# AdaLN-FFN kernel on one core: x of tiles 2 and 3 loaded ahead of the first product's weights, the mixing weights made per block, and the first phase's lists in that order

## The chip, the cores and the metric

The kernel runs on one core of a Trainium2 chip. The metric is the device time of one execution in microseconds (us). TensorE is called PE here, VectorE DVE, ScalarE ACT, GpSimd POOL and the engine that starts most transfers SP. PE runs at one of two clocks, 1.2 or 2.4 GHz; the profile gives the granted one as a share of 2.4 GHz.

## The reference

```
x = x + L0_ffn(L0_cond(x, cond, weight, c_weight, fside), ffn_weight)
x = x + L1_ffn(L1_cond(x, cond, W0, b0, W1, b1, W2, b2, weight, bias_k), kernel, scale)

L0_cond: grouped convolution over 512 positions (32 channels, 4 groups, 9 taps),
         plus cond @ c_weight.T, plus fside, one value for a channel
L0_ffn:  rows and weights rounded to int8 by their largest magnitude, product
         [.., 512] x [512, 512], times both scales
L1_cond: att = softmax(gelu(gelu(cond @ W0 + b0) @ W1 + b1) @ W2 + b2)   # 64 x 8
         agg_w = einsum('bk,koi->boi', att, weight)                      # 64 x 32 x 32
         out = einsum('boi,bih->boh', agg_w, x) + (att @ bias_k)[:, :, None]
L1_ffn:  scale * (out @ (kernel * 2 - 1)),  [512, 512] signs
```

x is 64 x 32 x 512 in float32, 4 MB, and so is the result.

## The kernel before

The 64 samples are worked on in 16 tiles `t` of four samples each, 128 rows of 512. A tile goes through these steps: convolution on PE (`conv`, line 361, always for two tiles at once, in five `conv_step`s of 16 matmuls), bias on ACT (`convolved`, L759), largest magnitudes and scales on DVE (`maxima` L606, `scales` L615 to L629), rounding on POOL (`quantise`, L862), turning on PE (`turn_tile`, L381) and a copy on ACT (`quantised`, L765), the int8 product on PE (`ffn0_tile`, L389), scaling on DVE (`dequantise`, L636), the sum with x on POOL (`first_sum`, L875), the mixing over channels on PE (`mix_tile`, L396) and its bias on DVE (L644), a split into a high and a low part (ACT L771, POOL L881), the product with the signs on PE (`ffn1_tile`, L404 and L407), the result on DVE (L651) and the store.

A first phase comes ahead of the loop. It makes the convolution's weights, the two small gelu layers (`hidden1`, `hidden2`), the softmax (`logits`, `attention`), the int8 weights of the first product (`ffn0_weights(a)` for a = 0 to 3: load, DVE L554, POOL L853, PE L313, ACT L737), their scales (`ffn0_scales`, L321 and L567), and `mix`, which holds for each tile a 128 x 128 matrix with four 32 x 32 blocks of `agg_w` on its diagonal. In the same phase the tiles 0 to 3 are convolved, and tiles 0 and 1 go on to `dequantise`. The loop `for t in range(4, NT + 5)` follows; on PE it begins with the convolution of tiles 4 and 5, behind waits for all copies into `mix`.

Every engine works its list in the order in which the code is written, and waits on semaphores. So the order of the calls sets what stands behind what. A load of x for a tile is two transfers, `load_x(t, 0)` and `load_x(t, 1)`, of 256 KB each (the second is the same data shifted by one position), `load_q(a)` is one of 256 KB.

In the kernel before, `mixing_weights` on PE is eight matmuls (L338) of a 128 column piece of `mixk` with all 64 columns of `att_T`. Their result stands in PSUM with the output channels spread over all 128 partitions, and is taken to `mix` in sixteen copies of 32 x 128: eight on DVE (L599) and, through a copy `agg_sb` by ACT (L748), eight on POOL (L898).

## Time and profile before

| | us |
|---|---|
| median of three runs | 126.05 (125.63 to 126.14) |
| the profiled execution, its own time | 127.2 |
| its span in the trace | 125.2 |
| PE busy | 114.5 (91% of the span) |
| DVE, ACT, POOL busy | 76.0, 41.9, 70.6 |
| granted PE clock, mean over the span | 0.944 |

All times of the trace are counted from the span's start. The own time of an execution is 2.0 us longer than its span. A float32 matmul is recorded as two passes, so 16 matmuls are 32 records, each with its own weight load. Some records of matmuls are missing, so an "x151" in the chain stands for 160 passes.

### The profile page before, as it was taken

To read this page: it belongs to the slowest core of one execution; us is meant where nothing else is said; L and a number is where in the kernel's file an instruction comes from. 1 tells how busy PE (TensorE), PEld (TensorE's weight loads), DVE (VectorE), ACT (ScalarE), POOL (GpSimd) and SP (SyncE) were. 2 spreads that over 40 slices of the span, in tenths; PEclk is the share of its full clock that TensorE was granted. 3 is DMA by queue.
4 is the path that set the end of the run, shared out by engine and by line. 5 is a ranking of instruction groups with operands and counts; after the bars stand their busy time and mean duration, and the time that the engine had idled before them with its cause. 6 is when DMAs were issued, how large, how long until landed. Compare 5 with 4: busy or idle time off the path is not lost.

```text
span 125.2 us, 4314 instructions
## 1 busy us (share of the span) xinstructions
PE 114.5 (91%) x1759; PEld 77.2 (62%) x1759; DVE 76.0 (61%) x189; ACT 41.9 (33%) x81; POOL 70.6 (56%) x102
## 2 busy tenths in 40 slices
PE   4978999998998894999999999999999998699990
PEld 1345545653665562677768667777777684587880
DVE  6270578825965990078819855982987278275532
ACT  0414154355357402524083126406331722420210
POOL 6970047557974776007852882677088407975640
PEclk9999559589999999599999999999999999999999
DMA  1898999995999988309394731505132251021024
GB/s 42 220 200 304 222 232 216 205 220 124 228 225 224 228 178 242 73 14 284 105 260 135 216 118 58 168 5 169 67 109 93 80 163 56 32 84 63 25 99 153
DMA packets 11378, 18.60 MB, mean 149 GB/s; under 512 B 1624, under 2 KB 2776, under 8 KB 11360
## 3 DMA queue, kind: packets, MB, share of 16 engines
q1 hardware_dynamic: 10512, 17.84, 54.0%
q10 hardware_dynamic: 560, 0.44, 1.9%
q8 instruction: 14, 0.23, 0.9%
q0 software_dynamic: 288, 0.06, 0.4%
q14 instruction: 4, 0.03, 0.1%
HBM read 14.12 MB, written 4.19 MB: 146 GB/s over the span
## 4 chain that ended last, share of the span: by engine, by line
PE 77%; DVE 6%; DMA 5%; issue 4%; ACTq 2%; POOL 2%; ACT 2%; POOLq 0%; DVEq 0%
PE ps L361 21%; PE ps L404 13%; PE ps L407 11%; PE ps L396 11%; PE ps L389 10%; DMA xs<-in_x_dram 5%; PE ps L381 4%; DVE q_max L554 2%; PE ps L338 2%; DVE mix L599 1%; PE ps L321 1%; ACT xq L765 1%; POOL x L875 1%; PE ps L313 1%; PE ps L423 1%
## 5 line engine op out<-in xcount | busy, mean ns | idle before, releaser
L875 POOL TENSOR_TENSOR x<-xr,delta 128x512 f32<-128x512 f32 x16 | 18.7, 1168 | 29.8 <-DVE delta L636 29.1
L361 PE MATMUL ps<-xs,conv_st 32*32 32x256 f32 x1280 | 31.5, 424 | 3.2 <-issue 1.8
L361 PEld LDWEIGHTS ps<-xs,conv_st 32*32 32x32 f32 x1280 | 17.3, 106 | 10.9 <-issue 5.4
L881 POOL TENSOR_TENSOR z_lo<-z,z_hi 128x512 fp32r<-128x512 f32 x16 | 20.4, 1277 | 4.7 <-ACT z_hi L771 3.7
L606 DVE TENSOR_REDUCE row_max<-ysb 128x2 f32<-128x512 f32 x16 | 10.8, 678 | 18.3 <-ACT ysb L759 18.3
L771 ACT ACTIVATE z_hi<-z 128x512 fp32r<-128x512 f32 x16 | 10.1, 631 | 32.5 <-DVE z L644 32.3
L404 PE MATMUL ps<-sign,z_hi 128*128 128x512 f32 x60 | 18.3, 428 | 0.4 <-ACT aggb_bc L752 0.4
L396 PEld LDWEIGHTS ps<-mix,x 128*128 128x128 f32 x128 | 16.6, 191 | 2.8 <-POOL x L875 0.6
L389 PE MATMUL ps<-wq,xq 128*128 128x512 f16 x64 | 16.6, 381 | 0.9 <-DVE delta L636 0.5
L396 PE MATMUL ps<-mix,x 128*128 128x128 f32 x128 | 17.1, 276 | 0.1
L759 ACT ACTIVATE ysb<-ps,bias_col 128x256 f32<-128x256 f32 x32 | 13.3, 479 | 10.4 <-PE ps L361 10.3
L765 ACT ACTIVATE xq<-ps,half_col 128x512 f16<-128x512 f32 x16 | 11.0, 685 | 16.8 <-PE ps L381 16.7
L862 POOL TENSOR_SCALAR rounded<-ysb,c_inv 128x256 f32<-128x256 f32 x32 | 14.8, 482 | 3.1 <-DVE c_inv L622 3.1
L407 PE MATMUL ps<-sign,z_lo 128*128 128x512 f32 x60 | 16.2, 392 | 0.0
L651 DVE SCALAR_TENSOR_TENSOR res<-ps,scale_col,x 128x512 f32<-128x512 f32 x15 | 11.2, 746 | 7.9 <-PE ps L407 7.5
L636 DVE SCALAR_TENSOR_TENSOR delta<-ps,a_scale,w_scale 128x512 f16<-128x512 f32 x16 | 11.9, 743 | 2.8 <-PE ps L389 2.5
L407 PEld LDWEIGHTS ps<-sign,z_lo 128*128 128x128 f32 x60 | 11.3, 188 | 2.6
L404 PEld LDWEIGHTS ps<-sign,z_hi 128*128 128x128 f32 x60 | 10.7, 199 | 2.2 <-ACT aggb_bc L752 0.5
L644 DVE TENSOR_TENSOR z<-ps,aggb_bc 128x512 f32<-128x512 f32 x16 | 10.9, 681 | 1.5 <-PE ps L396 1.0
L389 PEld LDWEIGHTS ps<-wq,xq 128*128 128x128 f16 x64 | 5.0, 98 | 9.0 <-issue 4.6
L289 PE MATMUL ps<-ones_h 128*128 128x512 f16 x19 | 6.7, 509 | 1.7 <-DVE ones_h L515 1.7
L853 POOL TENSOR_SCALAR q_round<-q_raw,q_inv 128x512 f32<-128x512 f32 x4 | 2.7, 695 | 9.3 <-DVE q_inv L563 9.3
(108 smaller groups left out, 100.3 us busy)
## 6 DMA issues: line engine op xcount, KB each, us to landing
xs<-in_x_dram SPq DMA_DIRECT2D x31, 256.0 KB, 5.1
xr<-in_x_dram SPq DMA_DIRECT2D x16, 256.0 KB, 3.9
out_dram<-res SPq DMA_DIRECT2D x15, 256.0 KB, 2.0
q_raw<-in_L_ffn_weight_dram SPq DMA_DIRECT2D x4, 256.0 KB, 3.5
xs<-in_x_dram ACTq DMA_DIRECT2D x1, 256.0 KB, 6.3
sign_raw<-in_L_ffn_kernel_dram SPq DMA_DIRECT2D x1, 256.0 KB, 8.0
out_dram<-res SPq DMA_DIRECT2D x2, 128.0 KB, 1.7
w_sb<-in_L_cond_W_dram ACTq DMA_DIRECT2D x2, 64.0 KB, 4.8
```

What stands on the lines that cost most here:

```text
L361: mm = pe.matmul(Y[r][C * j:C * (j + 1), HL * qs[0]:HL * (qs[-1] + 1)], conv_st[C * r:C * (r + 1), m].rearrange("k o p -> k (o p)"), xs[C ...
L389: mm = pe.matmul(ACC, xq[:, t % 2, P * c:P * (c + 1)], wq[:, c, :], start=(c == 0), stop=(c == LC - 1))
L396: mm = pe.matmul(Z[:, P * c:P * (c + 1)], x1[:, t % NX1, P * c:P * (c + 1)], mix[:, t, :], start=True, stop=True)
L404: pe.matmul(FIN, z_hi[:, t % NH, P * c:P * (c + 1)], sign[:, c, :], start=(c == 0), stop=False)
L407: mm = pe.matmul(FIN, z_lo[:, t % NH, P * c:P * (c + 1)], sign[:, c, :], start=False, stop=(c == LC - 1))
L636: dve.scalar_tensor_tensor(out=delta[:, t % 2, :], in0=ACC, scalar=a_scale[:, t:t + 1], in1=w_scale[:], op0=ALU.mult, op1=ALU.mult).then_i ...
L651: dve.scalar_tensor_tensor(out=res[:, t % 4, :], in0=FIN, scalar=scale_col[:, 0:1], in1=x1[:, t % NX1, :], op0=ALU.mult, op1=ALU.add).then ...
L759: act.activation(ysb[:, t % 4, g, :], Y[2 * (t % 2) + g][:, HL * (t // 2 % 2):HL * (t // 2 % 2 + 1)], ACT.Identity, bias=bias_col[:, g, t: ...
L765: act.activation(xq[:, t % 2, :], TURN, ACT.Identity, bias=half_col[:, 0:1])\
L862: last = nc.gpsimd.tensor_scalar(rounded[:, t % 4, g, :], ysb[:, t % 4, g, :], c_inv[:, q, h, g:g + 1], ROUND, ALU.mult, ALU.add)
L875: nc.gpsimd.tensor_tensor(x1[:, t % NX1, :], xr[:, t % 4, :], delta[:, t % 2, :], ALU.add)\
L881: nc.gpsimd.tensor_tensor(z_lo[:, t % NH, :], z[:, t % 2, :], z_hi[:, t % NH, :].bitcast(F32), ALU.subtract)\
```

## The change

The same arithmetic is done in another form and order:

- SP loads x of tiles 0 to 3 first (eight transfers) and the weights of the first product behind them; `load_x(1, 1)` moves from ACT's queue to SP's. The rows for the sum and the signs come later. Three small loads (`fside`, `w2`, `b2`) move from POOL's queue to ACT's.
- `mixing_weights` on PE becomes, for each of four blocks b, 32 matmuls of 32 weight columns and 16 moving columns, whose results stand on the 32 partitions on which `mix` wants them. A block is then one copy of 32 x 512: blocks 0 and 1 on ACT, 2 and 3 on DVE. `agg_sb` and POOL's copies are gone.
- PE makes the small layers ahead of the first convolution, instead of between its steps, and all four `ffn0_weights` behind the second one; DVE, ACT and POOL have their lists in that order.
- The warm-up matmuls of PE are 13 instead of 19.

```diff
-    WARM = (11, 6, 2)
+    WARM = (8, 1, 1, 2, 1)
@@ SP
+            load_x(1, 1)
             sp.wait_ge(x_in[0][0][0], 32)
+            load_x(2, 0)
+            load_x(2, 1)
+            sp.wait_ge(x_in[0][0][1], 32)
+            load_x(3, 0)
+            load_x(3, 1)
             load_q(0)
+            sp.wait_ge(x_in[0][1][0], 32)
             load_q(1)
             load_q(2)
...
+            sp.wait_ge(x_in[0][1][1], 32)
             load_q(3)
...
@@ PE
-            def mixing_weights(hs):
+            def mixing_weights(b):
+
                 pe.wait_ge(mixk_in, 16)
-                for h in hs:
-                    mm = pe.matmul(FIN[:, B * h:B * (h + 1)],
-                                   mixk[:, OL * h:OL * (h + 1), :].rearrange("k o c -> k (o c)"), att_T[:],
-                                   start=True, stop=True)
-                if h == OH - 1:
-                    mm.then_inc(agg_mm, 1)
+                for o in range(C):
+                    mm = pe.matmul(FIN[C * b:C * (b + 1), NT * o:NT * (o + 1)], mixk[:, o, :], att_T[:, b:B:NB],
+                                   start=True, stop=True, tile_position=(0, C * b))
+                mm.then_inc(agg_mm, 1)
...
-            mixing_weights(range(0, 4))
+            mixing_weights(0)
+            mixing_weights(1)
             conv_inputs(0, [1])
             conv_step(0, [1], 0)
-            mixing_weights(range(4, OH))
-            ffn0_weights(2)
             conv_step(0, [1], 1)
-            ffn0_weights(3)
-            ffn0_scales()
+            mixing_weights(2)
             conv_step(0, [1], 2)
-            pe.wait_ge(wq_ready, LC)
+            pe.wait_ge(ident_h_ready, 2)
             turn_tile(0)
             conv_step(0, [1], 3)
+            conv_step(0, [1], 4).then_inc(conv_done, 1)
+            mixing_weights(3)
             turn_tile(1)
+            for a in range(LC):
+                ffn0_weights(a)
+            ffn0_scales()
+            pe.wait_ge(wq_ready, LC)
             ffn0_tile(0)
-            conv_step(0, [1], 4).then_inc(conv_done, 1)
             ffn0_tile(1)
             pe.wait_ge(wsc_ready, 1)
             spread_bias(0)
             pe.wait_ge(agg_copied, 2)
-            pe.wait_ge(agg_spread, 2 * NB)
+            pe.wait_ge(agg_in, 2)
@@ DVE
             mixing_weights(2)
             ffn0_scales()
+            maxima(2)
+            maxima(3)
             dve.wait_ge(wsc_ready, 1)
             dequantise(0)
+            scales(2, 2)
+            dequantise(1)
             mixing_weights(3)
-            dequantise(1)
-            maxima(2)
-            maxima(3)
-            scales(2, 2)
@@ ACT
-            ffn0_weights(0)
-            ffn0_weights(1)
-            ffn0_weights(2)
-            ffn0_weights(3)
-            mixing_weights()
-            quantised(0)
-            quantised(1)
-            convolved(2, 0)
...
+            mixing_weights(0)
+            quantised(0)
+            convolved(2, 0)
...
+            quantised(1)
+            ffn0_weights(0)
+            ffn0_weights(1)
+            ffn0_weights(2)
+            ffn0_weights(3)
+            mixing_weights(1)
```

On PE, from the last step of the small layers to the first product, the list before reads (L361 are the convolution's steps, L338 the mixing weights, L313 the turns of the int8 weights, L381 those of the tiles, L389 `ffn0_tile`):

```order
L289 MATMUL ps<-ones_h 128x512 x2
L333 MATMUL ps<-mixb,att_T 64x32
L338 MATMUL ps<-att_T,mixk 128x64 x4
L361 MATMUL ps<-xs,conv_st 32x256 x16
L338 MATMUL ps<-att_T,mixk 128x64 x4
L313 MATMUL ps<-ident_h,q_round 128x128 x4
L361 MATMUL ps<-xs,conv_st 32x256 x16
L313 MATMUL ps<-ident_h,q_round 128x128 x4
L321 MATMUL ps<-ident,q_max 128x128 x4
L361 MATMUL ps<-xs,conv_st 32x256 x16
L381 MATMUL ps<-ident_p,rounded 128x8x16 x4
```

In the changed kernel the same place on PE reads (L356 are the steps, L335 the mixing weights, L376 the turns of the tiles, L309 those of the weights, L317 the scales, L384 `ffn0_tile`):

```order
L329 MATMUL ps<-mixb,att_T 64x32
L335 MATMUL ps<-att_T,mixk 32x16 x64
L356 MATMUL ps<-xs,conv_st 32x256 x32
L335 MATMUL ps<-att_T,mixk 32x16 x32
L356 MATMUL ps<-xs,conv_st 32x256 x16
L376 MATMUL ps<-ident_p,rounded 128x8x16 x4
L356 MATMUL ps<-xs,conv_st 32x256 x32
L335 MATMUL ps<-att_T,mixk 32x16 x32
L376 MATMUL ps<-ident_p,rounded 128x8x16 x4
L309 MATMUL ps<-ident_h,q_round 128x128 x16
L317 MATMUL ps<-ident,q_max 128x128 x4
L384 MATMUL ps<-wq,xq 128x512 x8
```

The eight wide mixing matmuls are 128 narrow ones, and the sixteen turns of the int8 weights, which stood in three places among the steps, stand together behind the last narrow one.

On DVE, from the copy of the int8 weights' scales to the end of the first phase, the list before reads (L567 `ffn0_scales`, L636 `dequantise`, L599 copies into `mix`, L606 `maxima`):

```order
L567 COPY w_scale<-ps 128x512
L636 SCALAR_TENSOR_TENSOR delta<-ps,a_scale,w_scale 128x512
L599 COPY mix<-ps 32x16x8 x4
L636 SCALAR_TENSOR_TENSOR delta<-ps,a_scale,w_scale 128x512
L606 TENSOR_REDUCE row_max<-ysb 128x2 x2
```

and in the changed kernel (L562, L599 now `maxima`, L629 `dequantise`, L608 to L622 `scales(2, 2)`, L593 the copy into `mix`):

```order
L562 COPY w_scale<-ps 128x512
L599 TENSOR_REDUCE row_max<-ysb 128x2 x2
L629 SCALAR_TENSOR_TENSOR delta<-ps,a_scale,w_scale 128x512
L608 STREAM_SHUFFLE row_swap<-row_max 128x4
L610 SCALAR_TENSOR_TENSOR row_both<-row_max,row_swap 128x4
L613 TENSOR_SCALAR c_scale<-row_both 128x4
L615 RECIPROCAL c_inv<-c_scale 128x4
L617 STREAM_SHUFFLE n_scale<-c_scale 128x4
L619 TENSOR_SCALAR n_high<-n_scale,low_high 128x2
L622 SCALAR_TENSOR_TENSOR a_scale<-n_scale,low_high,n_high 128x2
L629 SCALAR_TENSOR_TENSOR delta<-ps,a_scale,w_scale 128x512
L593 COPY mix<-ps 32x16x32
```

The last copy into `mix`, for which PE waits ahead of the loop, stands behind both `dequantise` and the scales of tiles 2 and 3.

## Rows read from the trace of the kernel before

**Rows 1.** The granted clock of PE in 40 slices of 3.13 us, in tenths.

```profile
PEclk9999559589999999599999999999999999999999
```

**Rows 2.** The chain that ended last: start, us, what.

```profile
3.40 6.34 DMA xs<-in_x_dram
...
31.55 0.40 DVE mix L599
...
32.01 3.52 PE ps L361 x143
...
44.97 2.09 PE ps L361 x85
47.05 1.84 issue
48.89 2.61 PE ps L361 x60
...
59.32 0.89 PE ps L396 x8
60.22 3.45 PE ps L361 x150
...
71.57 3.46 PE ps L361 x151
```

**Rows 3.** Two stretches: busy us of each engine, granted clock, DMA share, GB/s.

```profile
12.30:17.30 5.00, 5.00 (x104) 2.62 (x104) 2.85 (x12) 0.95 (x4) 0.90 (x2) 0.50 0.98 219
45.00:60.20 15.20, 13.36 (x217) 9.17 (x221) 7.76 (x17) 4.16 (x8) 6.44 (x9) 0.89 0.59 155
```

**Rows 4.** Timeline of PE's weight loads: start, us, engine, line.

```profile
19.53 0.19 PEld L333 LDWEIGHTS ps<-mixb,att_T 8*64 8x64 f32 x2 [0.83 <-DVE att_T L586]
19.75 0.96 PEld L338 LDWEIGHTS ps<-att_T,mixk 8*128 8x128 f32 x8
20.78 0.23 PEld L361 LDWEIGHTS ps<-xs,conv_st 32*32 32x32 f32 x32
```

**Rows 5.** Durations in ns, min/median/max, of L333's and L338's weight loads.

```profile
L333 PEld LDWEIGHTS ps<-mixb,att_T x2: 128/130/131, 19.5 to 19.6; 8*64 8x64 f32 x2
L338 PEld LDWEIGHTS ps<-att_T,mixk x16: 181/187/187, 19.8 to 22.2; 8*128 8x128 f32 x16
```

**Rows 6.** Timeline of PE at the condition's product, L451.

```profile
11.60 0.43 PE L451 MATMUL ps<-cond_T,cond_wT 128*128 128x64 f32 x2
11.96 0.44 PE L453 MATMUL ps<-ones,fside_rep 1*128 1x64 f32 x2
```

**Rows 7.** Timeline of DVE around the end of the first phase.

```profile
26.35 0.69 DVE L567 COPY w_scale<-ps 128x512 f32<-128x512 f32 x1 [1.43 <-PE ps L321]
29.54 0.75 DVE L636 SCALAR_TENSOR_TENSOR delta<-ps,a_scale,w_scale 128x512 f16<-128x512 f32 x1 [2.50 <-PE ps L389]
...
32.64 1.27 DVE L606 TENSOR_REDUCE row_max<-ysb 128x2 f32<-128x512 f32 x2
34.02 0.01 DVE L615 LOAD_MASK_SELECT row_swap<-row_max  x1
...
36.29 0.32 DVE L629 SCALAR_TENSOR_TENSOR a_scale<-n_scale,low_high,n_high 128x2 f32<-128x2 f32 x1
```

**Rows 8.** Timeline of ACT: an int8 weight's copy and a turned tile's.

```profile
24.79 0.69 ACT L737 ACTIVATE wq<-ps,half_col 128x512 f16<-128x512 f16 x1 [0.95 <-PE ps L313]
...
28.62 0.69 ACT L765 ACTIVATE xq<-ps,half_col 128x512 f16<-128x512 f32 x1 [0.56 <-PE ps L381]
```

**Rows 9.** Issue and landing of w1, loaded by L724 of ACT.

```profile
L724 ACTq DMA_DIRECT2D w_sb<-in_L_cond_W_dram x1: 628/628/628, 2.7 to 2.7; - x1
...
DMA to landing us min/median/max: 5.9/5.9/5.9
```

**Rows 10.** Issue and landing of x of tile 3, second part.

```profile
L197 SPq DMA_DIRECT2D xs<-in_x_dram x1: 593/593/593, 12.1 to 12.1; - x1
...
DMA to landing us min/median/max: 8.0/8.0/8.0
```

More of the change, by code:

```diff
@@ L185, in slot, with mix_block, agg_block @@
             return t // 4 % NX
-        def mix_block(b, ol):
-            return mix[C * b:C * (b + 1), :, C * b + ol:C * (b + 1):OL]
-        def agg_block(b, ol, src=FIN):
-            return src[C * ol:C * (ol + 1), :].rearrange("p (o t b) -> p b t o", o=OH, b=NB)[:, b]
+        def mix_block(b):
+            return mix[C * b:C * (b + 1), :, C * b:C * (b + 1)]
+        def agg_block(b):
+            return FIN[C * b:C * (b + 1), :].rearrange("p (o t) -> p t o", t=NT)
         def load_shift(eng, t, s):
@@ L593, in mixed_bias, with mixing_weights @@
                    .then_inc(aggb_lo, 1)
-            def mixing_weights(ol):
+            def mixing_weights(b):
                 dve.wait_ge(mix_zeroed, 1)
-                dve.wait_ge(agg_mm, 1)
-                for b in range(NB):
-                    last = dve.tensor_copy(mix_block(b, ol), agg_block(b, ol))
-                last.then_inc(agg_copied, 1)
+                dve.wait_ge(agg_mm, b + 1)
+                dve.tensor_copy(mix_block(b), agg_block(b)).then_inc(agg_copied, 1)
             def maxima(t):
@@ L676, in _ @@
             dve.wait_ge(low_high_ready, 1)
+            softmax_first()
             conv_bias()
+            softmax_second()
+            attention_copy()
+            mixed_bias()
+            maxima(0)
+            maxima(1)
+            scales(0, 2)
             ffn0_maximum(0)
@@ L744, in exponentials, with mixing_weights @@
                                accum_out=att_s[:, 2:3]).then_inc(exp_ready, 1)
-            def mixing_weights():
-                act.wait_ge(agg_mm, 1)
-                act.activation(agg_sb[:], FIN[0:2 * C], ACT.Copy).then_inc(agg_in, 1)
+            def mixing_weights(b):
+                act.wait_ge(mix_zeroed, 1)
+                act.wait_ge(agg_mm, b + 1)
+                act.activation(mix_block(b), agg_block(b), ACT.Copy).then_inc(agg_in, 1)
             def spread_bias(n):
@@ L780, in _ @@
             convolved(1, 1)
+            mixing_weights(0)
+            quantised(0)
+            convolved(2, 0)
+            convolved(2, 1)
+            convolved(3, 0)
+            convolved(3, 1)
+            quantised(1)
             ffn0_weights(0)
@@ L850, in _, with ffn0_rounded @@
             nc.gpsimd.memset(mix[:], 0.0).then_inc(mix_zeroed, 1)
-            for a in range(LC):
+            def ffn0_rounded(a):
                 pool.wait_ge(q_inverted, a // 2 + 1)
@@ L890, in _ @@
             quantise(1)
-            pool.wait_ge(mix_zeroed, 1)
-            pool.wait_ge(agg_in, 1)
-            pool.wait_ge(quant_done, 2)
-            for ol in range(2):
-                for b in range(NB):
-                    need(pool, agg_spread, NB * ol + b)
-                    nc.gpsimd.tensor_copy(mix_block(b, ol), agg_block(b, ol, agg_sb)).then_inc(agg_spread, 1)
-            pool.wait_ge(agg_spread, 2 * NB)
+            for a in range(LC):
+                ffn0_rounded(a)
             first_sum(0)
-            signs(0)
             first_sum(1)
-            signs(1)
             quantise(2)
             quantise(3)
+            signs(0)
+            signs(1)
             for t in range(4, NT + 5):
```

71 lines of the change are left out of this document (23 added, 48 removed).

## The prediction

> **What bounds the kernel now.** I read the clock line first, then the chain that ended last, then the first phase engine by engine. PE is the engine to watch: it is busy in 91% of the span, and the chain is mostly PE. From 60.22 to 71.57 us two tiles pass in 11.35 us, and the chain there is PE with no gap [rows 2]. The change does not touch that loop, so its worth is the time at which the loop starts, and what state the engines are in then. The loop's first convolution starts at 32.01 us, behind a copy into `mix` that ends at 31.95 [rows 2]. The first convolution could not start before 9.74, when the fourth transfer of x landed (3.40 + 6.34) [rows 2]. So the first phase is the 22.3 us between. In it the clock stands at half in three of the 40 slices [rows 1], one stretch being 12.3 to 17.3 us [rows 3]. Behind it comes a loss that is not the first phase's: the two tiles from 44.97 to 60.22 take 15.25 us instead of 11.35, 3.9 us more. In them is a gap of 1.84 us in the middle of a convolution for which the profile names no cause ("issue") [rows 2], and a mean clock of 0.89 [rows 3].
>
> **The change, part by part.**
>
> *Transfers.* x of tile 3 landed at 12.1 + 8.0 = 20.1 us [rows 10], and before, PE began the convolution of tiles 2 and 3 right behind it: its loads start at 20.78 [rows 4]. With eight transfers of x first, the fourth landing again near 9.7, four more of 256 KB at some 220 GB/s [rows 3] (1.2 us each) land near 14.5, and the four of the int8 weights near 19. Bytes and queues are otherwise the same. This frees up to 5.6 us, but only if PE has nothing else to do. Next comes what PE has to do.
>
> *PE up to the first convolution's end.* The small layers now stand ahead of it. `hidden2` waits for w1, which landed at 2.7 + 5.9 = 8.6 us [rows 9] and is loaded as before. Behind it stand a warm-up matmul, the condition's eight passes at 0.37 us for two (11.60 to 11.96 [rows 6]), 1.5 us, and the second gelu with the logits, some 0.7: the convolution starts near 11.6 instead of 9.9 and ends, at 3.5 us for 160 passes (the 3.52 of the loop's [rows 2]), near 15.1. That needs the full clock.
>
> *The mixing weights.* Before: 16 passes. Now 128 matmuls, so 256 passes, each with a weight load of 32 columns and 16 moving columns. No row shows this form. The nearest: loads of 128 columns follow each other at (0.96 - 0.187) / 7 = 0.110 us, loads of 64 columns at 0.19 - 0.131 = 0.06 [rows 4, 5]. That is 0.025 less for 32 columns less, so a straight line gives 0.035 for 32 columns. The bounds: 0.06 (nothing gained by halving the columns again) and 0.022, the convolution's pass over many tiles of the array, 3.52 / 160 [rows 2]. I take 0.035: 256 x 0.035 = 9.0 us. The moving columns seem to cost nothing beside the load: `mix_tile` with 128 of them has 0.89 / 8 = 0.111 us for a pass [rows 2], L338 with 64 the same 0.110 [rows 4, 5]. The Trainium skill's "TensorE: Matmul & The Clock Gate", section "Part 3: Packing small matmuls", says otherwise: a weight load overlaps a running matmul only if their row groups differ, and all 128 narrow matmuls stand in row group 0. These rows show an overlap within one row group, so the trace does not bear it out; by the rule the 9.0 us would be nearer the upper bound.
>
> *PE up to the int8 weights, T.* From 15.1: mixing bias 0.3, mixing weights 9.0, the second convolution 3.5, two `turn_tile` 0.7, and 0.5 that I allow for changing between narrow and other matmuls. T = 29.1 us. x of tiles 2 and 3 and the int8 weights on POOL are ready long before. So the earlier x hides behind the mixing weights; if these cost nothing, T would be 20.1.
>
> *From T to the loop.* What stood in several places now stands in a row. ACT: `quantised(1)` and four weight copies, 5 x 0.69 = 3.45 us [rows 8]; two pairs of turns on PE wait for them in turn, `ffn0_scales` runs beside. So `ffn0_tile(0)` ends near T + 4.4. DVE meanwhile: the scales' copy from T + 3.3 for 0.69, then both `maxima`, 1.27 [rows 7], to T + 5.3. They are ahead of `dequantise(0)`, 0.75: T + 6.0. Then `scales(2, 2)`, which took from 34.02 to 36.61, 2.6 us [rows 7]; then `dequantise(1)` 0.75 and the last copy into `mix`, 512 elements, as long as the copy of that size in L567, 0.7: T + 10.05. PE has long finished `ffn0_tile(1)` and waits at that copy; everything of the loop is queued behind. The loop starts at 29.1 + 10.05 = 39.15 us, 7.1 later. The copies saved (sixteen of 128 elements for four of 512) are off this path, but for the last.
>
> *The clock at the start.* PE waits nearly 3 us there. Before, behind the gap of 1.84 us the clock was low, and the two tiles lost 3.9 - 1.84 = 2.1 us beyond the gap. I take 1.0 of this for the loop's restart, between 0 and 2.1, since `ffn0_tile(1)` is inside the wait.
>
> *The loss from 45 to 60 us.* The gap has no cause in the rows. The page counts 16 KB packets of instructions beside it, and the changed kernel has 234 more matmul passes on PE (240 for mixing, 6 warm-ups less), so whatever falls there falls elsewhere. I cannot say whether the 3.9 us stay; I take half off, -1.9, bounds 0 and -3.9.
>
> *Warm-ups, moved small loads:* nothing; they stand ahead of 9.7 us, covered by the transfer of x. Without that cover the moved loads would cost ACT's queue three issues of 0.6 us.
>
> Sum: +7.1 + 1.0 - 1.9 = +6.2 us. The profiled execution took 127.2 us by its own time and would go to 133.4; the median was 126.05, and I forecast from that: 132.3 us.
>
> **Rivals.**
>
> *No overlap (0.15).* The narrow passes go at 0.06 us, each load waiting for the multiply ahead of it (the skill's rule above), or at the low clock. Price: 256 x 0.025 = 6.4 us more: 138.7. For it: these matmuls use 8 rows and 32 columns of the array, and the low clock in [rows 3] came in a stretch of small ones. Against: the equal spacing of the two wide forms.
>
> *Cheap passes, slower all the same (0.13).* 0.022 a pass: 3.3 us less: 129.0. For it: the same 32 x 32 shape in the convolution. Against: that one spreads over sixteen tiles, this one stays in one. "TensorEngine Tiling (Array Packing)", section "Instruction Overhead", of the Trainium skill gives about 60 cycles as the least for a matmul; by an estimate from it 256 passes at 2.4 GHz are 6.4 us, near this rival. No row here shows it.
>
> *The early loss goes whole (0.07).* Everything is ready when a later loop starts, and the other 2.0 us of the 3.9 vanish too: 130.3, slower still.
>
> *Faster (0.05).* The narrow passes run at the rate at which the convolution's 32 loads were taken, 0.23 / 32 = 0.007 us [rows 4]. They then cost 1.8 us, T is 21.9, the loop starts at 31.95 and the sum is -0.1 + 1.0 - 1.9 = -1.0: 125.05. It decides from 0.011 us a pass down (6.2 us / 256 = 0.024 below my 0.035). Against: those loads only filled a queue; the step itself went at 0.022.
>
> **How the numbers follow.** The forecast, slower by 3.5 to 10 us with the mixing passes and the serial end as causes, has 0.57; its own range is 129.5 to 136. The rivals have 0.15, 0.13, 0.07 and 0.05; 0.03 is left for no measurable difference, gains and losses cancelling. The range: passes from 0.022 to 0.06 us are -3.3 and +6.4, the clock -1.0 and +1.1, the early loss +1.9 and -2.0, and a low clock over the first convolution +2. Not all come together: 128 to 138. About 0.5% is what a measurement of this kernel can tell from no change. Slower by more: 0.57 + 0.15 + 0.13 + 0.07 = 0.92. Faster 0.05, same 0.03.
>
> **What would show it.** In the profile after: 256 passes of L335, 0.035 us apart, in blocks of 64 or 128; the second convolution waiting for no transfer; the turns L309 starting near 29 us; PE idle for some 3 us ahead of the first L356 of the loop, ended by DVE's copy L593; that L356 at 39 us; then 11.35 us for two tiles. The prediction is wrong if the narrow passes are far from 0.035 us, if DVE's row of maxima, scales and copy is much shorter than 6.8 us from the scales' copy on, or if the clock falls for long stretches of narrow matmuls.

## The result, and the profile after

| | before | after |
|---|---|---|
| median of four runs | 126.05 us (125.63 to 126.14) | 141.73 us (140.39 to 143.12) |
| the profiled execution, its own time | 127.2 | 141.91 |
| its span | 125.2 | 140.0 |
| granted PE clock, mean | 0.944 | 0.890 |
| passes on PE | 1759 | 1993 |

The changed kernel takes 1.1216 times as long (95% interval 1.1132 to 1.13): by the medians 15.7 us more, where I had forecast 6.2. The median lies 3.7 us above the range. Ratios in this document leave out executions that took over 1.5% more than the fastest of the same kernel. The profiled execution of the kernel before was 1.2 us above its median, that of the changed kernel 0.2, so what is read from the two traces adds up to 14.7 us; the other 1.0 stands in none of the terms below.

The clock line of the page, 40 slices of 3.5 us, answers to [rows 1]:

```profile
PEclk9999995555555569999999999999999999999999
```

The low clock is one block now: from 20.8 to 51.5 us, nine slices, where three stood scattered in the first phase and one near 50 us. The windows put numbers on it (busy us of each engine, granted clock, DMA share, GB/s), as [rows 3] did before:

```profile
17.30:22.70 5.40, 5.40 (x160) 4.92 (x151) 3.49 (x15) 2.16 (x5) 2.15 (x5) 0.82 0.65 150
22.70:37.10 14.40, 13.53 (x304) 10.66 (x302) 3.80 (x11) 2.94 (x6) 3.54 (x6) 0.50 0.84 227
37.10:48.10 11.00, 8.29 (x33) 4.44 (x33) 5.91 (x15) 3.72 (x6) 1.85 (x2) 0.50 0.28 78
48.10:53.30 5.20, 5.20 (x162) 3.54 (x162) 0.00 (x0) 0.35 (x1) 4.33 (x7) 0.68 0.94 210
53.30:73.70 20.40, 19.68 (x267) 14.23 (x271) 13.78 (x30) 9.31 (x19) 11.07 (x13) 1.00 0.36 104
```

In the second window PE is busy for 13.53 of 14.40 us and gets half the clock. So this is no engine that waits: it works all the time, slowly. Only in the third does it wait, 2.7 us of 11. The timeline of PE (start, us, line, shape, passes, wait) shows the same row by row:

```profile
9.42 0.63 PE L284 MATMUL ps<-ones_h 128*128 128x512 f16 x1
...
10.31 0.69 PE L447 MATMUL ps<-ones,fside_rep 1*128 1x64 f32 x2
...
12.47 4.53 PE L356 MATMUL ps<-xs,conv_st 32*32 32x256 f32 x128
...
17.12 0.77 PE L356 MATMUL ps<-xs,conv_st 32*32 32x256 f32 x32
...
18.05 4.85 PE L335 MATMUL ps<-att_T,mixk 8*32 8x16 f32 x125
...
24.83 3.42 PE L335 MATMUL ps<-att_T,mixk 8*32 8x16 f32 x61
...
32.11 3.58 PE L335 MATMUL ps<-att_T,mixk 8*32 8x16 f32 x64
35.62 0.60 PE L376 MATMUL ps<-ident_p,rounded 128*128 128x128 f16 x4
37.10 1.01 PE L309 MATMUL ps<-ident_h,q_round 128*128 128x128 f16 x8 [0.87 <-ACT xq L760]
...
39.52 2.02 PE L317 MATMUL ps<-ident,q_max 128*128 128x128 f32 x8
```

The two passes of L447, beside the condition's product, take 0.69 us, where the same row (L453) took 0.44 in [rows 6]; a 512-column warm-up takes 0.63 us. So the clock is at half there already, although the page shows 9 in those slices (its clock record begins at 17.3 us). The mean of 0.890 counts these 17.3 us as full, the 0.944 of the kernel before only the first 5.4 us; so such means can't be compared from run to run.

The first 128 narrow passes take 4.78 us in the chain, 0.037 us each, which looks like my 0.035. But the clock fell inside them, at 20.75 us. The window over L335, cut there:

```profile
18.12:20.75 2.63, 2.63 (x88) 2.63 (x89) 1.00 0.44 87
20.75:22.90 2.15, 2.15 (x46) 2.15 (x42) 0.50 0.74 179
```

At the full clock 88 passes take 2.63 us, 0.030 each; the 40 behind them take 2.15 us, 0.054 each (the counts of a window also hold passes that began ahead of it). The last 64 go at 0.053 too (3.36 us for 63 in the chain). The 0.037 is a mixture of the two; so are the "0.037 us (full clock)" and "0.037 us at the full clock" in two expectations below.

The end of the first phase, on DVE, answers to [rows 7]:

```profile
42.18 1.27 DVE L599 TENSOR_REDUCE row_max<-ysb 128x2 f32<-128x512 f32 x2
43.37 0.74 DVE L629 SCALAR_TENSOR_TENSOR delta<-ps,a_scale,w_scale 128x512 f16<-128x512 f32 x1
...
44.30 1.06 DVE L610 SCALAR_TENSOR_TENSOR row_both<-row_max,row_swap 128x4 f32<-128x4 f32 x1
...
46.58 0.74 DVE L629 SCALAR_TENSOR_TENSOR delta<-ps,a_scale,w_scale 128x512 f16<-128x512 f32 x1
47.35 0.70 DVE L593 COPY mix<-ps 32x512 f32<-32x512 f32 x1
```

The row of maxima, scales and copy is as forecast, in kind and within some tenths in length. The chain from there answers to [rows 2]:

```profile
47.35 0.71 DVE mix L593
48.06 0.04 issue
48.10 4.80 PE ps L356 x154
...
62.34 3.47 PE ps L356 x143
...
73.72 3.40 PE ps L356 x142
77.11 0.06 issue
77.17 0.65 PE ps L356 x6
```

The loop starts at 48.10 instead of 32.01, 16.1 us later. Its first convolution takes 4.80 us, most of it at the low clock. Then two tiles pass in 11.38 us, from 62.34 to 73.72: the gap of 1.84 us that stood in the second loop before is not there. From the loop's start to its third convolution it is 25.6 us, where it was 28.2: -2.6. Behind it, 1.3 us come back, most of them in two convolutions that take 4.17 (at 73.65) and 3.97 us (at 108.36) instead of 3.5. 16.1 - 2.6 + 1.3 = 14.8, the difference of the two spans.

### The profile page after: what moved, and what is told of

Same layout as the page of the kernel before. It is cut to its first block, busy times and chain, and to the rows that moved or that the text cites. A ratio compares the mean times of both kernels' runs of the same rounds, so it can differ in the third digit from the quotient of the medians.

```text
span 140.0 us, 4772 instructions
## 1 busy us (share of the span) xinstructions
PE 129.1 (92%) x1993; PEld 91.5 (65%) x1993; DVE 74.3 (53%) x183; ACT 42.5 (30%) x82; POOL 65.8 (47%) x91
## 4 chain that ended last, share of the span: by engine, by line
PE 83%; DMA 4%; DVE 3%; issue 3%; ACT 2%; POOL 2%; ACTq 1%; POOLq 0%; DVEq 0%
PE ps L356 24%; PE ps L399 11%; PE ps L402 10%; PE ps L391 10%; PE ps L384 9%; PE ps L335 8%; DMA w_sb<-in_L_cond_W_dram 4%; PE ps L376 3%; PE ps L317 1%; PE ps L309 1%; ACT xq L760 1%; PE ps L447 1%; POOL x L869 1%; DVE row_both L610 1%; PE ps L418 1%
## 5 line engine op out<-in xcount | busy, mean ns | idle before, releaser
L356 PE MATMUL ps<-xs,conv_st 32*32 32x256 f32 x1280 | 35.3, 466 | 1.3 <-DVE mix L593 1.3
L356 PEld LDWEIGHTS ps<-xs,conv_st 32*32 32x32 f32 x1280 | 21.1, 114 | 9.9 <-issue 3.0
L384 PE MATMUL ps<-wq,xq 128*128 128x512 f16 x64 | 18.3, 412 | 1.5 <-DVE delta L629 1.2
L599 DVE TENSOR_REDUCE row_max<-ysb 128x2 f32<-128x512 f32 x16 | 10.8, 681 | 16.6 <-ACT ysb L754 16.6
L760 ACT ACTIVATE xq<-ps,half_col 128x512 f16<-128x512 f32 x16 | 11.0, 685 | 25.6 <-PE ps L376 25.6
L399 PE MATMUL ps<-sign,z_hi 128*128 128x512 f32 x60 | 17.6, 415 | 0.4 <-ACT aggb_bc L747 0.4
L856 POOL TENSOR_SCALAR rounded<-ysb,c_inv 128x256 f32<-128x256 f32 x32 | 14.8, 481 | 3.7 <-DVE c_inv L615 3.7
L335 PEld LDWEIGHTS ps<-att_T,mixk 8*32 8x32 f32 x256 | 12.2, 137 | 0.7 <-issue 0.5
L384 PEld LDWEIGHTS ps<-wq,xq 128*128 128x128 f16 x64 | 5.4, 103 | 10.8 <-issue 6.8
L335 PE MATMUL ps<-att_T,mixk 8*32 8x16 f32 x256 | 12.2, 201 | 0.0
L629 DVE SCALAR_TENSOR_TENSOR delta<-ps,a_scale,w_scale 128x512 f16<-128x512 f32 x16 | 11.9, 742 | 0.3
L399 PEld LDWEIGHTS ps<-sign,z_hi 128*128 128x128 f32 x60 | 10.2, 189 | 2.1 <-ACT aggb_bc L747 0.5
```

Of the source, the lines that this page charges most:

```text
L335: mm = pe.matmul(FIN[C * b:C * (b + 1), NT * o:NT * (o + 1)], mixk[:, o, :], att_T[:, b:B:NB], start=True, stop=True, tile_position=(0, C ...
L356: mm = pe.matmul(Y[r][C * j:C * (j + 1), HL * qs[0]:HL * (qs[-1] + 1)], conv_st[C * r:C * (r + 1), m].rearrange("k o p -> k (o p)"), xs[C ...
L384: mm = pe.matmul(ACC, xq[:, t % 2, P * c:P * (c + 1)], wq[:, c, :], start=(c == 0), stop=(c == LC - 1))
L399: pe.matmul(FIN, z_hi[:, t % NH, P * c:P * (c + 1)], sign[:, c, :], start=(c == 0), stop=False)
L629: dve.scalar_tensor_tensor(out=delta[:, t % 2, :], in0=ACC, scalar=a_scale[:, t:t + 1], in1=w_scale[:], op0=ALU.mult, op1=ALU.mult).then_i ...
L760: act.activation(xq[:, t % 2, :], TURN, ACT.Identity, bias=half_col[:, 0:1])\
```

## The experiments

The kernel before, run beside them on the same chips, had medians of 126.5, 126.5 and 126.3 us in the three sets. In what follows "from the changed kernel" and "from the kernel before" say where an edit begins.

The first set asks whether the clock at the start, the shape of the mixing passes or their number carries the loss.

**More warm-ups, from the changed kernel.**

```diff
-    WARM = (8, 1, 1, 2, 1)
+    WARM = (11, 1, 1, 2, 1)
```

> The changed kernel with eleven warm-up matmuls at the start instead of eight, all else as it is. In the changed kernel's trace every 512 column matmul of the first 10 us took 0.63 us, and the first convolution 5.3 us instead of 3.5. Theory 'early warm-ups': the missing three are why the clock stayed at half until 17.3 us; with eleven the clock is full near 5.5 us as in the kernel before, the first convolution takes 3.5 to 4.5 us and the time falls by 1.5 to 3 us, to 139 to 140. Theory 'narrow matmuls': the stretch at half from 20.8 to 51.5 us stays as it is, since the narrow matmuls cause it; if the early warm-ups were the cause of all, that stretch would go too and the time fall to 132 to 134.

142.59 us, ratio 1.132 (1.118 to 1.147): no gain, where 1.5 to 3 us were expected. Yet the clock was full from 5.4 us on and the narrow passes began 3 us earlier, at 15.04. They then stopped for 1.32 us ("issue", 19 passes in), the clock fell at 19.1, and the turns of tile 0 began at 29.4, as in the changed kernel (29.59). What is won ahead of the narrow passes is lost in them.

**Fewer warm-ups, from the kernel before.**

```diff
-    WARM = (11, 6, 2)
+    WARM = (8, 6, 2)
```

> The kernel before with eight warm-up matmuls at the start instead of eleven. Theory 'early warm-ups': the clock stays at half beyond 5.4 us here too; ahead of 9.7 us that is hidden behind the load of x, behind it the convolution's first steps are slower: 0.5 to 2 us more, 126.5 to 128. Rival: the six matmuls that follow at 7 us raise the clock anyway, and the time is within 0.3 us of 126.05.

125.67 us, ratio 1.003 (0.997 to 1.008). The fewer warm-ups cost nothing by themselves.

**The eight wide matmuls back, from the changed kernel.**

```diff
-                for o in range(C):
-                    mm = pe.matmul(FIN[C * b:C * (b + 1), NT * o:NT * (o + 1)], mixk[:, o, :], att_T[:, b:B:NB],
-                                   start=True, stop=True, tile_position=(0, C * b))
-                mm.then_inc(agg_mm, 1)
+                if b == 0:
+                    for h in range(OH):
+                        mm = pe.matmul(FIN[:, B * h:B * (h + 1)],
+                                       mixk[:, OL * h:OL * (h + 1), :].rearrange("k o c -> k (o c)"), att_T[:],
+                                       start=True, stop=True)
+                    mm.then_inc(agg_mm, NB)
```

> The changed kernel, but block 0 of the mixing weights issues the kernel before's eight wide matmuls and blocks 1 to 3 issue none; copies, order and loads as changed. The values in the mixing matrices stand in wrong places, the work on them is the same. Theory 'narrow matmuls': 256 passes (12 us of PE) go for 16 (2 us), and the clock is full for most of the first phase, so the loop starts near 48.1 - 10 - 5 = 33 us or a little later (the serial end stays) and the time is 126 to 130. Rival 'serial order': the clock stays low because PE waits so often for ACT and DVE; then only the 10 us of passes go, less what x would now be waited for: 132 to 134.

133.06 us by the median, 8.7 less, within the rival's range. The four runs took 130.20, 132.36, 133.76 and 134.13 us; against the fastest it is 11.5 less. The timeline of PE in the run of 133.76:

```profile
18.73 1.99 PE L336 MATMUL ps<-att_T,mixk 8*128 8x64 f32 x16
...
29.02 1.01 PE L309 MATMUL ps<-ident_h,q_round 128*128 128x128 f16 x8 [1.92 <-ACT xq L762]
...
40.03 5.59 PE L358 MATMUL ps<-xs,conv_st 32*32 32x256 f32 x160 [2.42 <-DVE mix L595]
```

The mixing takes 2 us instead of 11.4, and the loop starts at 40.0 instead of 48.1. The rest of the loss stays, and so does a low clock, from 22.1 to 35.7 us and again over the loop's first convolution, which takes 5.59 us. So a low clock doesn't need the narrow matmuls. The run of 130.2 us has a mean clock of 0.973, the other three 0.88 to 0.90; but a mean counts what lies ahead of the first record as full, and the run of 130.2 has no trace, so that the clock makes this difference isn't shown.

**The narrow matmuls alone, from the kernel before.** They stand in the two places of the wide ones.

```diff
-                    mm = pe.matmul(FIN[:, B * h:B * (h + 1)],
-                                   mixk[:, OL * h:OL * (h + 1), :].rearrange("k o c -> k (o c)"), att_T[:],
-                                   start=True, stop=True)
+                    for o in range(C // 2 * (h % 2), C // 2 * (h % 2 + 1)):
+                        b = h // 2
+                        mm = pe.matmul(FIN[C * b:C * (b + 1), NT * o:NT * (o + 1)], mixk[:, o, :], att_T[:, b:B:NB],
+                                       start=True, stop=True, tile_position=(0, C * b))
```

> The kernel before, with the eight wide mixing matmuls replaced by the 128 narrow ones in the same two places, 64 in each; its sixteen copies stay, so the values stand in wrong places. Theory 'narrow matmuls': 240 passes more at 0.037 us (full clock) to 0.053 (half) are 9 to 13 us, all on the chain, and the clock falls behind them: 136 to 141. Rival 'serial order': the narrow passes cost their 9 us and no clock, 134 to 135, or less where they fill waits.

135.56 us, ratio 1.074 (1.057 to 1.092): 9.1 more, without any of the rest of the change. A window of it over the narrow passes, then two rows of PE:

```profile
19.20:33.90 14.70, 14.04 (x290) 13.57 (x288) 2.78 (x13) 0.11 (x1) 4.02 (x8) 0.52 0.93 192
```

```profile
19.19 6.29 PE L340 MATMUL ps<-att_T,mixk 8*32 8x16 f32 x125
...
32.54 1.46 PE L340 MATMUL ps<-att_T,mixk 8*32 8x16 f32 x24 [0.66 <-issue]
```

PE works for 14.04 of 14.70 us and has a granted clock of 0.52; before, between 17.3 and 32 us, it was 0.82. The first 125 passes go at 0.050 us. This is the term "mixing weights" measured alone. The time lies between the ranges of the two theories; the low clock, from 19.8 to 40.2 us, is what the first one said. The loop starts at 44.3, 12.3 later, and the early loss is gone as in the changed kernel: 3 us come back.

The second set asks what makes a narrow pass dear (its one array tile, or the clock), and what the end of DVE's list and the late weights are worth.

**The narrow matmuls in the four column groups in turn, from the changed kernel.**

```diff
-                for o in range(C):
-                    mm = pe.matmul(FIN[C * b:C * (b + 1), NT * o:NT * (o + 1)], mixk[:, o, :], att_T[:, b:B:NB],
-                                   start=True, stop=True, tile_position=(0, C * b))
-                mm.then_inc(agg_mm, 1)
+                if b == 0:
+                    for o in range(C):
+                        for j in range(NB):
+                            mm = pe.matmul(FIN[C * j:C * (j + 1), NT * o:NT * (o + 1)], mixk[:, o, :], att_T[:, j:B:NB],
+                                           start=True, stop=True, tile_position=(0, C * j))
+                    mm.then_inc(agg_mm, NB)
```

> The changed kernel with the same 128 narrow matmuls, all issued in the place of block 0, and in an order in which four following ones stand in the four column groups of the array (block inner, channel outer). In the changed kernel the passes of one block follow each other at 0.037 us at the full clock and 0.053 at half, always in one column group. Theory 'serial in one tile': matmuls in different column groups overlap, the 256 passes take 256 x 0.022 = 5.6 us or less instead of 12.2, and the time falls by 5 us or more, to 134 to 137. Rival 'load rate in one row group': weight loads of one row group do not overlap each other, a pass costs its 0.037 to 0.053 in any order, and the time stays within 2 us of 141.7.

142.19 us, ratio 1.129 (1.119 to 1.139): no gain, for a reason that I had not expected. PE in it:

```profile
17.61 0.38 PE L337 MATMUL ps<-att_T,mixk 8*32 8x16 f32 x22
18.84 1.83 PE L337 MATMUL ps<-att_T,mixk 8*32 8x16 f32 x128 [0.86 <-issue]
22.57 1.62 PE L337 MATMUL ps<-att_T,mixk 8*32 8x16 f32 x106 [1.90 <-issue]
24.04 1.12 PE L358 MATMUL ps<-xs,conv_st 32*32 32x256 f32 x21
27.65 3.27 PE L358 MATMUL ps<-xs,conv_st 32*32 32x256 f32 x75 [2.49 <-issue]
```

A pass costs 1.83 / 128 = 0.014 us, nearly all of it at half clock (it fell at 19.0 us), where it took 0.053 in one tile at that clock. But PE stands still three times, 5.25 us in all, and between two stops lie 128 passes each time (128, then 106 + 21 with one record missing). A pass is two instructions, a load and a multiply, so that is 256 instructions, and the page counts 16 KB instruction packets. It looks as if PE worked its instructions off faster than they come; the last experiment below settles it.

**Wide warm-ups between the narrow ones, from the changed kernel.** One matmul of 512 columns behind every eight.

```diff
-                mm.then_inc(agg_mm, 1)
+                    if o == C - 1:
+                        mm.then_inc(agg_mm, 1)
+                    if o % 8 == 7:
+                        warm(1, ACC)
```

> The changed kernel with a 512 column warm-up matmul behind every eight narrow ones, sixteen in all, which adds 3.4 us of PE work at the full clock. Theory 'low activity': the clock fell at 20.8 us because the narrow matmuls keep little of the array active; the fillers hold it up, the first phase's later half runs at the full clock, and the time falls by 2 to 6 us in spite of the work added, to 136 to 140. Rival 'waits': the clock is low because of the waits on ACT and DVE from 36 to 48 us and the fillers only cost: 144 to 147.

147.84 to 154.88 us in three runs, with mean clocks of 0.83 to 0.88. The fourth, the profiled one, took 270.36 us and is left out: in its trace all of PE is slow, also the loop that the edit leaves alone (a pass of `ffn0_tile` takes 0.84 us on average, 0.41 in the changed kernel), and it has no clock record. So no trace shows the clock under the fillers. By the times they cost 6 us and more: they are no remedy.

**DVE's last copy and scales where they were, from the changed kernel.**

```diff
             mixing_weights(2)
+            mixing_weights(3)
             ffn0_scales()
-            maxima(2)
-            maxima(3)
             dve.wait_ge(wsc_ready, 1)
             dequantise(0)
-            scales(2, 2)
             dequantise(1)
-            mixing_weights(3)
+            maxima(2)
+            maxima(3)
+            scales(2, 2)
```

> The changed kernel with DVE's last copy into mix right behind the one of block 2, and the maxima and scales of tiles 2 and 3 behind both dequantise, as in the kernel before. Theory 'serial end on DVE': PE waited 1.0 us for the first delta and 1.3 us more at the end for the copy; both go, the loop starts near 45.8 instead of 48.1 and the time falls by 2 to 3 us, to 139 to 140. Rival: the scales, later now, hold up the turns of tiles 2 and 3 in the loop, and what is won is given back: within 0.7 us of 141.7.

138.8 us, ratio 1.100 (1.091 to 1.109): 2.9 less. PE ahead of the loop, and its first convolution:

```profile
43.30 1.02 PE L384 MATMUL ps<-wq,xq 128*128 128x512 f16 x4 [0.99 <-DVE delta L629]
44.26 0.50 PE L344 MATMUL ps<-aggb_row,ones_r 2*128 2x512 f32 x1
44.69 3.53 PE L356 MATMUL ps<-xs,conv_st 32*32 32x256 f32 x160
```

PE no longer waits for a copy into `mix`. The loop starts 3.4 us earlier and its first convolution takes 3.53 us instead of 4.80. Of the 3.4 us, 0.9 were there ahead of the part that the edit touches: the last turn of a tile ended at 35.3 instead of 36.2. The wait for the first delta, which was to go too, is still there (0.99).

**Only the order of the loads, from the kernel before.**

```diff
             sp.wait_ge(x_in[0][0][0], 32)
+            load_x(2, 0)
+            load_x(2, 1)
+            sp.wait_ge(x_in[0][0][1], 32)
+            load_x(3, 0)
+            load_x(3, 1)
             load_q(0)
+            sp.wait_ge(x_in[0][1][0], 32)
             load_q(1)
             load_q(2)
-            sp.wait_ge(x_in[0][0][1], 32)
+            sp.wait_ge(x_in[0][1][1], 32)
             load_q(3)
-            load_x(2, 0)
-            sp.wait_ge(q_in[0], 16)
-            load_x(2, 1)
-            sp.wait_ge(q_in[1], 16)
-            load_x(3, 0)
-            sp.wait_ge(q_in[2], 16)
-            load_x(3, 1)
```

> The kernel before with only the order of the loads on SP changed: x of tiles 2 and 3 ahead of the four loads of the first product's weights, which then land near 19 us instead of 12.8. Theory 'the weights are late next': the turns of the int8 weights stood at 17.3 us on PE, behind them attention and the mixing weights; PE waits for the rounding, which ends 4 to 6 us later, and the loop starts 3 to 5 us later: 129 to 131. Rival: the second convolution, which waited for x until 20.1 us, was as close a limit, and the two cancel: 125.5 to 127.

128.27 us, ratio 1.020 (1.012 to 1.027): 1.8 more. PE waits for the rounded int8 weights:

```profile
19.32 0.39 PE L312 MATMUL ps<-ident_h,q_round 128*128 128x128 f16 x4 [3.86 <-POOL q_round L852]
...
36.36 3.49 PE L360 MATMUL ps<-xs,conv_st 32*32 32x256 f32 x160
```

The loop starts 4.35 us later; as the early loss is gone here too, 1.8 are left. x of tiles 2 and 3 in time brings nothing by itself, and the int8 weights behind it are late for a list that wants them.

The third set puts remedies together and repeats the supply question in the kernel before.

**Wide matmuls and DVE's old end together, from the changed kernel** (the edits of "eight wide matmuls" and "DVE's last copy").

> The changed kernel with two parts undone: the eight wide mixing matmuls (values in wrong places) and DVE's last copy and scales as in the kernel before. Alone the first took 8.7 us off and the second 2.9. Theory 'three separate causes': they add, 133.1 - 2.9 = 130 us, and some 4 us stay that belong to the late int8 weights and their place behind everything. Rival 'shared cause, the low clock': with fewer waits the clock recovers earlier too, more than the sum goes, and the time is 127 to 128.5.

127.45 us (126.09 to 128.12), 14.3 less than the changed kernel; the ratio to before is 1.019, with an interval of 0.977 to 1.061 that tells little. The clock line, and the loop's start:

```profile
PEclk9999997798699999999999999999999999999999
```

```profile
35.47 3.54 PE L358 MATMUL ps<-xs,conv_st 32*32 32x256 f32 x160
```

By medians the two edits alone were worth 8.7 and 2.9, together they are worth 14.3. The excess of 2.7 hangs on the three slower runs of the wide matmuls alone. Against its run of 130.2 us there is none: 11.5 and 2.9 make 14.4. So the runs don't show that the two parts work on each other. Nor do the mean clocks show a cause: of the four runs here the one of 126.09 us has 0.945, the one of 127.28 us 0.973.

**The same with the int8 weights loaded, rounded and turned early.** On SP and in PE's `ffn0_weights`:

```diff
-            load_x(2, 0)
-            load_x(2, 1)
-            sp.wait_ge(x_in[0][0][1], 32)
-            load_x(3, 0)
-            load_x(3, 1)
             load_q(0)
-            sp.wait_ge(x_in[0][1][0], 32)
             load_q(1)
             load_q(2)
-            sp.wait_ge(x_in[0][1][1], 32)
+            sp.wait_ge(x_in[0][0][1], 32)
             load_q(3)
+            load_x(2, 0)
+            sp.wait_ge(q_in[0], 16)
+            load_x(2, 1)
+            sp.wait_ge(q_in[1], 16)
+            load_x(3, 0)
+            sp.wait_ge(q_in[2], 16)
+            load_x(3, 1)
@@ PE, ffn0_weights
-                pe.wait_ge(xq_ready, 2)
```

On PE `ffn0_weights(a)` and `ffn0_scales` stand ahead of the second convolution, and DVE, POOL and ACT have their parts as early.

> As the run before, and the int8 weights taken forward: their loads ahead of x of tiles 2 and 3 on SP, their maxima ahead of attention on DVE, their rounding first on POOL, their turns, copies and scales right behind the mixing matmuls on PE and ACT. Theory 'late weights': this undoes the rest of the loss, and the time is 126 to 127.5. Rival: x of tiles 2 and 3 is late instead, as much as the weights were, and it stays at 129 to 130.

125.06 us (ten runs, 123.75 to 126.43), ratio 1.000 (0.994 to 1.007): 2.4 less again, level with the kernel before. PE in it:

```profile
19.55 1.04 PE L309 MATMUL ps<-ident_h,q_round 128*128 128x128 f16 x8
...
32.36 3.51 PE L358 MATMUL ps<-xs,conv_st 32*32 32x256 f32 x160
```

The loop starts at 32.4, as before. With this the whole loss is accounted for by three parts that can be taken out: the narrow matmuls, DVE's end and the late int8 weights (with PE's wait for `xq_ready`), each with whatever low clock goes with it.

**Narrow matmuls in turn over the column groups, from the kernel before.**

```diff
-                    mm = pe.matmul(FIN[:, B * h:B * (h + 1)],
-                                   mixk[:, OL * h:OL * (h + 1), :].rearrange("k o c -> k (o c)"), att_T[:],
-                                   start=True, stop=True)
+                    for o in range(OL * h, OL * (h + 1)):
+                        for j in range(NB):
+                            mm = pe.matmul(FIN[C * j:C * (j + 1), NT * o:NT * (o + 1)], mixk[:, o, :], att_T[:, j:B:NB],
+                                           start=True, stop=True, tile_position=(0, C * j))
```

> The kernel before with 128 narrow mixing matmuls in the two places of the eight wide ones, 64 in each, four following ones in the four column groups (values in wrong places). With one column group at a time this place cost 9.1 us. In the changed kernel the interleaved passes went at 0.014 us, but PE stood still without a recorded cause every 128 passes, 0.9 to 2.5 us each time. Theory 'instructions come too slowly': two such gaps come here too, and the time is 129.5 to 132. Rival: the gaps were of that place alone; then the passes cost 256 x 0.014 - 2.1 = 1.5 us more than the wide ones, and the time is 127 to 128.

133.07 us, ratio 1.065 (1.040 to 1.090): 2.5 less than with the narrow ones block by block, by medians, inside the spread of the two. The stops come here too:

```profile
31.63 0.52 PE L340 MATMUL ps<-att_T,mixk 8*32 8x16 f32 x24 [3.88 <-issue]
```

3.88 us for nothing that the timeline names, behind passes that went at 1.90 / 128 = 0.015 us, at half clock. Cheap passes are paid for in stops.

**Only DVE's last copies earlier, from the kernel before** (`mixing_weights(3)` ahead of the scales and `dequantise(0)`), to see whether the end of the first phase has to do with the gap behind it.

```diff
             mixing_weights(2)
+            mixing_weights(3)
             ffn0_scales()
             dve.wait_ge(wsc_ready, 1)
             dequantise(0)
-            mixing_weights(3)
             dequantise(1)
```

> The kernel before with DVE's four copies of mixing_weights(3) right behind those of mixing_weights(2), in a wait of 1.4 us that DVE had there, instead of between the two dequantise. The loop's first convolution, which waited for them until 31.95 us, would wait for nothing behind spread_bias, at 31.85. Theory 'DVE's copy hardly held the loop in the kernel before': 0 to 0.3 us less, no difference to be told. Rival: the state of the engines shifts by it and the gap at 47 us comes or goes, 1 to 3 us either way.

125.81 us, ratio 1.010 (1.000 to 1.021): nothing gained. The gap is still there:

```profile
50.81 1.97 PE L361 MATMUL ps<-xs,conv_st 32*32 32x256 f32 x70 [1.56 <-issue]
```

It stands before the last 70 of the 160 passes of the second loop's convolution. In the kernel before it stood at the same pass, which came 2.2 us earlier in time (47.05 against 49.25), and in the one with fewer warm-ups three passes later:

```profile
48.89 2.61 PE L361 MATMUL ps<-xs,conv_st 32*32 32x256 f32 x70 [1.84 <-issue]
```

```profile
49.98 2.40 PE L361 MATMUL ps<-xs,conv_st 32*32 32x256 f32 x67 [2.81 <-issue]
```

The second row is of the run with eight warm-ups, which has three passes fewer ahead of the loop. So the gap keeps its place in PE's instructions, not in time and not in the work.

The traces show what it is. Counted over all of PE's records (loads, multiplies and semaphore instructions), 449 stand ahead of the first stop of the matmuls in turn, 705 and 961 ahead of the next two, and 1473 ahead of the gap of the kernel before: 256 apart, or twice that. All 17 stops of PE that the timelines of all runs put down to "issue" lie on this grid, to within one record. The queue "q8 instruction" brings one packet of 16 KB for each block of 256: 14 in the kernel before, 16 in the changed one. Beside each longer stop stands the packet of its block (us; the time between is rounded from the trace):

| run | stop | PE goes on at | packet had ended at | between |
|---|---|---|---|---|
| before | 1.84 | 48.89 | 47.54 | 1.34 |
| fewer warm-ups | 2.81 | 49.98 | 48.59 | 1.39 |
| DVE's copies earlier | 1.56 | 50.81 | 49.42 | 1.39 |
| narrow matmuls alone | 0.66 | 32.54 | 31.06 | 1.48 |
| more warm-ups | 1.32 | 17.14 | 15.62 | 1.51 |
| in turn, changed kernel | 0.86 | 18.84 | 17.19 | 1.65 |
| the same | 1.90 | 22.57 | 21.05 | 1.52 |
| the same | 2.49 | 27.65 | 26.23 | 1.43 |
| in turn, kernel before | 1.33 | 25.16 | 23.73 | 1.42 |
| the same | 3.88 | 31.63 | 30.20 | 1.43 |

Over all 196 such blocks in 14 traces PE never began one less than 1.30 us after its packet had ended, and where it stopped it began between 1.33 and 1.65 us after. So these stops are waits for instructions. In the changed kernel the packet of the block that stopped the kernel before had ended at 35.9 us, 14.4 us ahead of need: that is why the gap is gone. Why a packet comes late (in the kernel before its transfer began 8 us after PE had begun the block ahead) is not shown.

## Why the prediction was wrong

The direction and the causes named were right; the sizes failed. By the terms of the prediction, on the profiled executions (14.7 us measured, 6.2 forecast):

| term | forecast | measured | off by |
|---|---|---|---|
| end of the first convolution | 15.1 | 17.9 | +2.8 |
| mixing bias | 0.3 | 0.2 | -0.1 |
| 256 narrow passes | 9.0 | 11.4 | +2.4 |
| second convolution | 3.5 | 5.6 | +2.1 |
| turns of tiles, allowance | 1.2 | 1.1 | -0.1 |
| T | 29.1 | 36.2 | +7.1 |
| T to the loop | 10.05 | 11.9 | +1.8 |
| loop's first convolution | +1.0 | +1.3 | +0.3 |
| early loss | -1.9 | -3.9 | -2.0 |
| rest of the loop | 0 | +1.3 | +1.3 |

(The measured rows are sums from the chain; T is the end of the last turn of a tile.) The rows below T sum, with it, to +8.5, and 6.2 + 8.5 = 14.7.

- **The step that failed** is "That needs the full clock" in the part on PE up to the first convolution, and with it the use of full-clock rows for all that comes behind. I wrote the condition down and did not price it but for "+2" in the range. The first convolution began 0.9 us late behind small products at half clock and took 5.4 us, the second took 5.6, where I had set the 3.5 of the loop; and of the narrow passes only 88 of 256 ran at the full clock. These terms (+2.8, +2.1, and +2.4 for the narrow passes) are all of T's error. "Or at the low clock" stood in the rival of 138.7, but for the narrow passes alone; the low clock came for everything from 20.8 to 51.5 us. A fall of the clock for long stretches of narrow matmuls stood among my signs of being wrong, without a price.
- **0.035 us for a narrow pass** was too high for the full clock (0.030) and too low for half (0.050 to 0.054). At 0.030 the 256 passes would have taken 7.7 us, 1.3 less than forecast; that the average came out near the forecast in the first 128 (0.037) is chance. The straight line through loads of 128 and 64 columns gave 0.005 too much. The 0.5 us allowed for changing between forms had no row behind it, and the chain shows no time for it: the two turns took 0.54 and 0.55 us at half clock, where I had 0.7 for both. By itself, in the kernel before, the narrow form costs 9.1 us.
- **The rule of the page on packing** of the Trainium skill ("TensorE: Matmul & The Clock Gate", "Part 3: Packing small matmuls"), by which a load overlaps only where row groups differ, is contradicted more sharply by the matmuls in turn: all in row group 0, in different column groups, 0.014 us a pass against 0.053 in one tile at the same half clock. What counts in these runs is whether the next pass goes to another tile.
- **The earlier x hides behind the mixing weights:** right. The second convolution waits for nothing, and the order of the loads alone makes the kernel before slower by 1.8 us.
- **The serial end:** right in its mechanism. PE's wait ahead of the loop ends by the copy L593, and DVE's old order takes back 2.9 us. It was 1.8 us short, all of it ahead of the scales' copy, which began at T + 5.3 instead of T + 3.3: PE's first turn of a weight waits for ACT's `quantised(1)` (`xq_ready`, 0.87 us with PE idle), and at half clock the last eight turns take 1.17 us and the passes of L317 1.8. From the copy to the loop it is 6.5 us, where 6.75 were forecast, though one of the small operations of `scales(2, 2)` took 1.06.
- **The early loss** went whole, -3.9, the case that I gave 0.07. It also went in the kernel before with narrow matmuls and with x first. That I gave the whole of it a small chance was no knowledge: the gap was a wait for instructions, and whether one is met depends on when a block is reached and when its packet lands, which I had not looked at. Behind the gap the clock was low from 49.8 to 53.2 us, which makes most of the other 2.0 us. That the gap brought it is not shown: with fewer warm-ups a gap of 2.81 us has such a stretch behind it too, but the one of 1.56 us in the last experiment has none. Of the 1.3 us that come back, 1.1 are in the two longer convolutions.
- **The terms as a sum:** not refuted. The wide matmuls alone take out 8.7 by the median and 11.5 by the fastest run, the tail 2.9, both 14.3; so whether the parts add depends on which run of the first is taken.

What stays open: what exactly brings the clock down. It is low in stretches with a full PE (the narrow passes, 0.52) and in stretches in which PE waits (the wide matmuls, 22.1 to 35.7 us); three warm-ups more only moved the block forward (19.1 to 43.0 us), and wide fillers don't bring the time back.

## What to carry to other kernels

Before many small matmuls take the place of a few wide ones, price them at the low clock as well and price everything that stands behind them at it too: here the passes cost 2.4 us more than forecast, the convolutions with what stands ahead of them 4.9. Where a forecast says "that needs the full clock", give the term a second price at half clock. When a price is checked against a trace, cut the window where the clock changes: an average over both clocks can agree with a wrong price. A copy that lets the loop start belongs ahead of work that only the next tiles want, and spreading small matmuls over column groups is worth it only while PE's instructions come fast enough. A gap put down to "issue" in the middle of equal matmuls is worth a count of the instructions ahead of it and a look at the instruction packets beside it.

## What the runs showed of the hardware

- Narrow float32 passes (8 rows, 32 columns, 16 moving) cost 0.030 us each in one array tile at the full clock, 0.050 to 0.054 at half, and 0.014 to 0.015 at half clock when successive ones go to different column groups.
- At that rate PE stops every 128 passes, 256 instructions, for 0.86, 1.90 and 2.49 us, and in another kernel for 3.88. In all kernels here such stops end 1.33 to 1.65 us after the end of a 16 KB instruction packet. "Runtime: NRT & Kernel Launch", "Instruction fetch mechanics", of the Trainium skill says that instructions are refilled in blocks of 16 KiB, 256 instructions, at a cost that is "mostly hidden". The block's size agrees with the spacing of the stops; the cost is not hidden here, with the DMA engines busy in 0.78 of that stretch (17.6 to 27.7 us).
- The granted clock stood at half while PE was busy in 94% of the time (22.7 to 37.1 us of the changed kernel), and at 0.52 while it was busy in 96% (the narrow matmuls alone).
- The profile's clock line can show 9 where no clock record exists yet, and the mean counts it as full: matmuls of 512 columns took 0.63 us there, and 0.38 in the run with more warm-ups, at the full clock.
